# One transfer per slot for queries and keys, behind the position band, and a gate unit moved behind the last exponentials

## The reference, cut to what matters

```python
# attention, per sample: 384 tokens, 16 heads of 16 channels
q, k, v = shape((hn @ Wq + bq) * SCALING), shape(hn @ Wk + bk), shape(hn @ Wv + bv)
w = einsum('btd,bsd->bts', q, k) + rel_to_abs(einsum('btd,md->btm', q, rel_k))   # band: |t-s| <= 4
p = softmax(w, axis=-1)
o = p @ v + einsum('btm,md->btd', abs_to_rel(p), rel_v)
h = h + o.reshape(...) @ Wo + bo
# experts, per sample: 8 experts, all computed for every token
out = sum_e routing[:, e] * ((silu(x @ Wg[e]) * (x @ Wu[e])) @ Wd[e])
```

## Time and profile before

| | |
|---|---|
| median of the runs | 1242.7 us |
| the profiled execution, its own time | 1242.83 us |
| its span, first to last instruction | 1241.0 us |
| TensorE busy (matmul) | 1023.4 us, 82% |
| VectorE busy | 751.7 us, 61% |
| ScalarE busy | 451.2 us, 36% |
| queue of SP: data moved | 86.24 MB |

### The profile page before, as it was taken

One profiled execution on the slowest core, in us unless ns is written; L12 is line 12 of the kernel. 1 busy time (PEld: TensorE's weight loads), 2 busy tenths in 40 slices (PEclk: granted clock), 3 DMA queues, 4 the chain that ended last, 5 costly groups with the idle time before them and its releaser, 6 DMA issues.

```text
span 1241.0 us, 16784 instructions
## 1 busy us (share of the span) xinstructions
PE 1023.4 (82%) x5668; PEld 745.0 (60%) x5668; DVE 751.7 (61%) x1605; ACT 451.2 (36%) x651; POOL 242.6 (20%) x262
## 2 busy tenths in 40 slices
PE   5446689879898898878898798888898888987798
PEld 4221378628785477636786287745786277762687
DVE  5466364865568556774648655675658746486443
ACT  1134313472235522453134723355124631247211
POOL 4258120040200311031200402013200312004000
PEclk9677799989999999999999999999999899998899
DMA  5394206302081203602062111802044020620100
GB/s 159 120 232 145 40 5 177 62 10 57 6 211 30 39 18 89 148 10 52 4 180 59 31 34 35 202 10 39 18 146 92 10 52 5 180 60 14 40 1 13
DMA packets 96962, 87.87 MB, mean 71 GB/s; under 512 B 67281, under 2 KB 85074, under 8 KB 95090
## 3 DMA queue, kind: packets, MB, share of 16 engines
q1 hardware_dynamic: 96524, 86.24, 28.2%
q0 software_dynamic: 384, 1.05, 0.3%
HBM read 60.35 MB, written 26.92 MB: 70 GB/s over the span
## 4 chain that ended last, share of the span: by engine, by line
PE 34%; issue 23%; DVE 19%; DMA 9%; SPq 5%; ACT 5%; POOL 4%; POOLq 0%; DVEq 0%; ACTq 0%
PE S L924 10%; DMA k_st<-d_parts 6%; DVE maxima L1233 5%; PE S L945 5%; SPq L573 4%; PE S L855 4%; PE S L838 4%; DVE S L1254 3%; PE S L790 3%; PE S L750 3%; ACT scratch L1045 3%; DVE res L1387 2%; PE S L666 1%; DMA txt_row<-in_L_txt_W_E,txt_idx 1%; DMA w_d<-in_L_ffn_Wg 1%
## 5 line engine op out<-in xcount | busy, mean ns | idle before, releaser
L1506 POOL TENSOR_TENSOR bands<-scratch,one 64x432 f32<-64x432 f32 x128 | 119.2, 931 | 529.0 <-ACT scratch L1045 523.4
L1082 ACT ACTIVATE silu<-S 128x384 f32<-128x384 f32 x128 | 62.9, 491 | 371.4 <-PE S L924 260.2
L1233 DVE TENSOR_REDUCE maxima<-S 128x2 f32<-128x768 f32 x192 | 172.7, 951 | 27.3 <-PE S L798 26.2
L945 PE MATMUL S<-w_d,hT 128*128 128x256 f32 x768 | 182.7, 382 | 1.5 <-DVE hT L1375 0.7
L1254 DVE TENSOR_TENSOR S<-S,bands 64x144 f32<-64x144 f32 x384 | 154.4, 402 | 48.1 <-PE S L838 37.5
L1045 ACT ACTIVATE scratch<-S 128x768 f32<-128x768 f32 x192 | 155.4, 811 | 60.4 <-DVE S L1254 45.1
L790 PE MATMUL S<-k_st,q_st 128*128 128x384 bf16 x384 | 102.7, 334 | 65.3 <-DVE maxima L1233 37.1
L945 PEld LDWEIGHTS S<-w_d,hT 128*128 128x128 f32 x768 | 142.4, 190 | 21.7 <-issue 2.3
L1375 DVE TENSOR_TENSOR hT<-silu,S 128x384 f32<-128x384 f32 x128 | 70.7, 552 | 118.6 <-PE S L924 96.9
L838 PE MATMUL S<-q_st,k_st 128*128 128x384 bf16 x384 | 99.9, 360 | 41.7 <-ACT scratch L1045 37.9
L838 PEld LDWEIGHTS S<-q_st,k_st 128*128 128x128 bf16 x384 | 25.8, 100 | 135.3 <-ACT scratch L1045 99.4
(11 more groups left out here) (167 smaller groups left out, 1510.7 us busy)
## 6 DMA issues: line engine op xcount, KB each, us to landing
bands<-d_band_s SPq DMA_DIRECT2D x16, 864.0 KB, 8.8
scratch<-d_band_t SPq DMA_DIRECT2D x8, 1632.0 KB, 8.2
d_parts<-scratch SPq DMA_DIRECT2D x48, 192.0 KB, 1.9
q_st<-d_parts SPq DMA_DIRECT2D x48, 192.0 KB
k_st<-d_parts SPq DMA_DIRECT2D x48, 192.0 KB
d_band_w<-bands SPq DMA_DIRECT2D x32, 240.0 KB, 3.8
out<-scratch SPq DMA_DIRECT2D x8, 384.0 KB, 2.6
x_in<-in_x SPq DMA_DIRECT2D x8, 256.0 KB, 3.3
```

Source lines behind the costliest of these rows:

```text
L945: mm = pe.matmul(D[:, i // 2, (i % 2) * E:(i % 2 + 1) * E], hT[:, (FT * e + m) % 3, i * P:(i + 1) * P], w_d[:, e, m, :], start=(m == 0), s ...
L1233: dve.tensor_reduce(dst, S[:, c0:c0 + 2, PAD:PAD + T], AX, ALU.max).then_inc(max_done.sem, 1)
L1506: nc.gpsimd.tensor_tensor(bands[rows, :, :, 2 * pair:2 * pair + 2].rearrange("p i w h -> p h i w"), win, one[rows].unsqueeze(2).unsqueeze( ...
```

## The change

Four things change. `q_st` and `k_st` become the two halves of one tile, and a slot's query row and key row come in one transfer, six instead of twelve. These six stand behind the load of the position band, no longer half in front of it. The last of the maxima items but one gets a unit behind it. Behind the first `values` tile of the last group, that is behind the last exponentials on ScalarE's list, stands a gate unit with a wait for bank 6 (`gate_bank`); FILL_OUT has two units less.

```diff
-FILL_MAXIMA = [0, 1, 1] + [0, 0, 1] * 7
+FILL_MAXIMA = [0, 1, 1] + [0, 0, 1] * 6 + [0, 1, 1]
-FILL_OUT = [("turn_outputs", 3), ("turn_attn", 6), ("turn_weights", 1), ("rel_values", 1)]
+FILL_OUT = [("turn_outputs", 3), ("turn_attn", 5), ("turn_weights", 1), ("rel_values", 0)]
...
-        q_st = sb("q_st", [P, AH, T], BF16)
-        k_st = sb("k_st", [P, AH, T], BF16)
+        qk_st = sb("qk_st", [P, 2, AH, T], BF16)
+        q_st, k_st = qk_st[:, 0], qk_st[:, 1]
...
             last = AH // GRP - 1
+            if ffn:
+                assert left[0][0] == "gate"
+                steps.append(("gate_bank",))
+                fill(1)
             steps += [("values", last, i, dict(seen)) for i in VALUE_TILES[1:]] + [("copy", last)]
...
-                def stack(st, base, order):
+                def stack():
+                    size = E * T
                     for n in range(SLOTS):
+                        q, k = Q_PART[n], 3 + K_PART[n]
                         sp.dma_start(
-                            st[NEG + n:P:G8].rearrange("p h t -> p (h t)"),
-                            d_parts[base + order[n]].rearrange("(d g) m t -> d (g m t)", d=AD)
+                            qk_st[NEG + n:P:G8].rearrange("p s h t -> p s (h t)"),
+                            dram(d_parts, q * size, (AH * T, AD), ((k - q) * size, 2), (1, AH * T))
                         ).then_inc(stacked.sem, 16)
...
                 sp.dma_start(q_st[0:NEG], d_zero).then_inc(stacked.sem, 16)
-                sp.wait_ge(q_out.sem, q_out.at(b, 3))
-                stack(q_st, 0, Q_PART)
+
 
                 sp.wait_ge(proj_pe.sem, proj_pe.at(b, 10))
                 sp.wait_ge(rel_t_out.sem, rel_t_out.at(b, P // BT))
@@ -601,8 +606,9 @@
+                sp.wait_ge(q_out.sem, q_out.at(b, 3))
                 sp.wait_ge(k_out.sem, k_out.at(b, 3))
-                stack(k_st, 3, K_PART)
+                stack()
...
+            def gate_bank(b):
+
+                pe.wait_ge(o_copied.sem, o_copied.at(b, AH // GRP - 1))
+
```

More of the change, by code:

```diff
@@ L278, in fusion_block @@
         q_out, k_out = sig("q_out", 3, 16), sig("k_out", 3, 16)
-        stacked = sig("stacked", 2 * SLOTS + 1, 16)
+        stacked = sig("stacked", SLOTS + 1, 16)
         rel_t_out, rel_s_out = sig("rel_t_out", P // BT, 16), sig("rel_s_out", TT, 16)
@@ L776, in maxima @@
                         pe.wait_ge(pool_consts, 8)
-                    pe.wait_ge(stacked.sem, stacked.at(b, 2 * SLOTS + 1))
+                    pe.wait_ge(stacked.sem, stacked.at(b, SLOTS + 1))
                     pe.wait_ge(v_done.sem, v_done.at(b, TT))
@@ L952, in _ @@
                         "project_v": project_v, "maxima": maxima, "weights_ready": weights_ready, "negate": negate,
-                        "negated": negated, "attend": attend, "values": values, "turn_weights": turn_weights,
+                        "negated": negated, "attend": attend, "gate_bank": gate_bank, "values": values, "turn_weights": turn_weights,
                         "turn_outputs": turn_outputs, "rel_values": rel_values, "turn_attn": turn_attn,
@@ L1018, in maxima @@
                     act.wait_ge(band_t_in.sem, band_t_in.at(b, 1))
+                    act.wait_ge(q_out.sem, q_out.at(b, 3))
                     act.wait_ge(k_out.sem, k_out.at(b, 3))
@@ L1225, in maxima @@
                     dve.wait_ge(band_t_in.sem, band_t_in.at(b, 1))
+                    dve.wait_ge(q_out.sem, q_out.at(b, 3))
                     dve.wait_ge(k_out.sem, k_out.at(b, 3))
```

## The result

The changed kernel takes 1251.93 us (median of 13 runs, 1245.32 to 1258.59), the kernel before 1243.44 us beside it (13 runs, 1239.78 to 1248.3). The ratio is 1.0061, 95% interval 1.0035 to 1.0087: slower, and above the range of the forecast. The profiled execution of after took 1252.16 us, with a span of 1250.2 us, 9.2 more than before.

What follows compares the result with a forecast made beforehand. TensorE, busy for 82% of the span, was taken as the bound. From 1242.8 us, a later start of +1.4 and moved units of -1.75 gave 1242.5 us, with a range of 1238 to 1248.

Steps and rivals of the forecast that it cites:

- The failed step: Loads ahead of the first maxima: reordering and joining leave the sum of queries, band and keys at 15.5 us.
- The third rival: Joined query and key rows move at 196 GB/s, 0.8 us longer a sample, ending at 1248.9 us; chance 0.12.
- The later start: The band, now first, waits for the last projection: issue 0.2 us later a sample, 1.4 us in seven, bounds 0 to 3.
- The units: Moved units around the attention: -0.25 us a sample, -1.75 us over seven, bounds -6 to +2 us.
- Three accumulations: On VectorE at the attention's start, three accumulations would precede the first band addition.
- the band addition: The first band addition, for item 0 at the attention's start, would begin 0.4 us sooner.
- d7a's idle: In the output part, TensorE would idle about 0.7 us between u15 and d7a in each sample.
- the idle ahead of the residual: TensorE's idle before the residual would be 1.35 us where it was 1.25, a loss of 0.1.
- the output part: Output side of the attention: changes sum to 0.05 us, with rounding 0.15 us a sample against the change.
- the gate unit fills no idle in its place: Behind the last group's first values tile there is no idle; TensorE's 1.56 us lie ahead and stay.
- The first rival: Each transfer costs 0.38 us of engine time, so six fewer save 2.3 us a sample: 1230.4 us; chance 0.08.
- The bound for no change: A measurement of this kernel tells about 0.3%, 3.7 us, from no change.

Runs made afterwards that it cites:

- e1_stack: Only the six joined transfers behind the band, with the old unit tables, against the kernel before: 1257.93 us, ratio 1.0122.
- e3_twelve_behind: Twelve separate transfers, all moved behind the band, with the old unit tables, against the kernel before: 1244.74 us, ratio 1.0025.
- f1_joined_alternate: The changed kernel with its joined transfers issued in slot order 2, 0, 3, 1, 4, 5: 1242.72 us, ratio 1.0015 to the kernel before.
- e4_cover: The changed kernel with two units (d3b, g9) moved ahead of the first maxima item: 1239.51 us, ratio 0.9992 to the kernel before.
- g4_best: Kernel before with new unit tables, gate unit ahead of the last group's first values tile, slot rows in every sixth partition: 1239.23 us, ratio 0.9985.
- e2_units: Only the moved units and the gate unit, twelve transfers in their old places, against the kernel before: 1238.65 us, ratio 0.9975.
- f4_gate_ahead: Moved units, twelve transfers in old places, gate unit ahead of the last group's first values tile: 1237.22 us, ratio 0.9966 to the kernel before.
- f3_units_cover: Moved units, twelve transfers in old places, two units (d3b, g9) ahead of the first maxima item: 1237.36 us, ratio 0.9963 to the kernel before.
- g1_neighbours: The changed kernel with a slot's 16 rows in 16 neighbouring partitions: 1323.56 us, ratio 1.0674 to the kernel before.
- g2_stride6: The changed kernel with a slot's 16 rows in every sixth partition: 1244.58 us, ratio 1.0032 to the kernel before.
- f2: The kernel before with the slots of both sixes issued in the order 2, 0, 3, 1, 4, 5: 1243.99 us, ratio 1.0021.

## Why the prediction was wrong

**The failed step** is "The queue is in order, so the sum is start + band + all rows [...] The sum of the three pieces stays, 15.5 us." The sum of the pieces did not stay: in sample 2 they take 17.3 us, the landing time grows by 0.79 us a sample, and 7 x 0.79 = 5.5 us were missing from the forecast. The time shows that joining does it: `e1_stack` has 1.0122, `e3_twelve_behind` 1.0025. Of the landing time 0.1 us go to the new place (17.86 to 17.99) and 0.3 to joining (18.33). The other 0.3 up to the 18.65 of after are between two executions of the same transfers. Why joined rows move more slowly stays open; `f1_joined_alternate` shows that another order of the slots is enough to take it back.

**The third rival had this with its price**, 196 GB/s and 0.8 us a sample; measured were 193 and 0.79. I gave it 0.12, for the reason that "the same 16 partitions are written by the same number of rows in both forms". The rows were compared one transfer at a time. Over several transfers the change also alters which partitions are written one after the other, and from which parts of DRAM the rows come; which of the two costs is not shown.

**What no rival had** is the clock. The rival ended at 1248.9, since it priced the longer wait by its length alone. The wait also brought TensorE to the lower level at the start of the maxima in four of seven samples, 1.2 us each; `e4_cover` took the wait away, and with it that fall and 0.7%. In the two traces of before and after it is set off by less time at the lower level behind the first band addition, so it isn't a loss that one can simply add to the landing. Which wait lets the clock fall stays open: in after it fell behind 3.10, 2.78, 2.26 and 2.06 us, and held behind 2.62, 2.50 and 2.03, and behind 2.58 in the last sample of before. Over the traces of all kernels here, samples 1 to 7, it held behind each wait up to 1.92 us at this place and fell behind each from 2.78 on; in between it did both (1.94 in `g4_best` and in `e1_stack`).

**The later start** was right in size. The last conversion on VectorE ahead of the last store starts at 346.98 and SP issues the band at 349.00, 2.02 behind it; before it was 1.85 (344.04 to 345.89), so 0.17 where 0.2 was said. From the residual on it is 0.20. `e3_twelve_behind`, the move alone, has 1.0025: 3.1 us (0 to 6.3), where 1.4 with bounds of 0 and 3 was said.

**The units** were right step by step. Three accumulations, the band addition 0.24 us sooner (0.4 said), d7a's idle 0.78 (0.7), the idle ahead of the residual up by 0.08 (0.1), the output part longer by 0.10 (0.15). These steps add up to 7 x (-0.24 + 0.10) = -1.0 us. `e2_units` measured -3.1 us, interval -6 to 0, where -1.75 was said; what its trace has beyond the steps is less time at the lower clock, a term that the forecast didn't have. So the size came near partly by luck. That the gate unit fills no idle in its place was right as well: 1.56 us are still there, and `f4_gate_ahead` halves them.

**The first rival** (each transfer costs engine time of its own, so that six fewer pay) is excluded. Six transfers fewer gave nothing: the wait grew. The Trainium skill (DMA: Bandwidth & Descriptors, Rules for kernel authors) advises to coalesce many small transfers and names 64 KB as the size under which a transfer is mostly overhead; these have 192 KB, and joining two and two cost 1% here. The section with the fixed cost that the forecast cites is on transfers issued from GpSimd; these come from SyncE, and no run here shows what such a cost would be.

**The bound for no change** was said to be 0.3%. Twelve runs of one of these kernels spread over 6 to 17 us, and their intervals are 0.2 to 0.3% to either side, so it was about right for the ratio. Only the intervals of after, `e1_stack`, `f3_units_cover`, `f4_gate_ahead`, `g1_neighbours` and `g2_stride6` leave out 1; `e2_units` and `e3_twelve_behind` can't be told from none.

## What to carry to other kernels

Fewer and larger transfers are not faster by themselves: when the DMA engines already read as busy throughout, look at the GB/s of the stretch and at which partitions consecutive transfers write, and try their order before their number. Where TensorE stands still for the landing, price a longer wait with a possible fall of its clock behind it, and put ready work into the wait; that was worth 0.7% here (`e4_cover`), nearly as much as going back to twelve transfers (0.9%, `e2_units` against after), and nothing that could be measured where the wait was short. A unit meant to fill a wait must stand ahead of the waiting instruction, not behind it. And when two orders of the work differ by a few microseconds, compare them at the same granted clock first.

## What was not expected of the hardware

- The rate of transfers with 16 partitions of 12288-byte rows depends on which partitions they are, and on the order of the slots in the queue, with the DMA share at 1.0 in all cases: 125 GB/s into 16 neighbouring partitions, 193 into every eighth, 234 in the first half of the rows when the slots of the two sets alternate.
- Packets that are faster by 8% (0.77 us instead of 0.83 in `f2`) did not land the stack sooner; the band's packets beside them spanned 6.7 us instead of 5.6.
- A wait of 2.06 us was followed by the lower clock once (1.94 in `g4_best`), while one of 2.62 us in another sample of the same execution was not.
- The lower clock turns up in other places from kernel to kernel: in after at the maxima, in `e1_stack` in the mixer (17.1 us between the residual and the next maxima where `e3_twelve_behind` has 6.8), and with the old unit tables more behind the first band addition (27.3 to 34.1 us against 17.1 to 23.9). So a loss of this kind is read from sums over the span and not from one place.
